# First attention of a four-layer network: dense masked products or nine shifted products on channel planes

## The reference

```python
def _unfold(x, k, dil):
    pad = dil * (k - 1) // 2
    xp = jnp.pad(x, ((0, 0), (0, 0), (pad, pad), (pad, pad)))
    return jnp.stack([xp[:, :, i * dil:i * dil + H, j * dil:j * dil + W] for i in range(k) for j in range(k)], axis=2)

def _dilate_attention(q, k, v, head_dim, scale, ksz, dil):
    qr = q.reshape(B, nh, head_dim, L)
    kp = _unfold(k, ksz, dil).reshape(B, nh, head_dim, kk, L)
    vp = _unfold(v, ksz, dil).reshape(B, nh, head_dim, kk, L)
    attn = jnp.einsum('bncl,bnckl->bnlk', qr, kp) * scale
    attn = jax.nn.softmax(attn, axis=-1)
    out = jnp.einsum('bnlk,bnckl->bnlc', attn, vp)
    ...
for g in range(G):                      # G = 4 groups of 48 channels
    qkv = jnp.einsum('oi,bihw->bohw', qkv_w, xg[g]).reshape(nd, 3, B, gd // 3, H, W)
    for i in range(nd):                 # dilations 1, 2, 3
        outs.append(_dilate_attention(qkv[i, 0], qkv[i, 1], qkv[i, 2], hd, scale, KSZ, DILATIONS[i]))
y = jnp.stack(outs).reshape(B, H, W, C)
return y @ proj_w.T + proj_b
```

## Time and profile before

| | us |
|---|---|
| runs of the kernel | 774.72, 776.76, 777.01 |
| median | 776.76 |
| span of the profiled execution | 779.2 |
| TensorE busy, share of the span | 707.0, 91% |
| VectorE, ScalarE, GpSimd busy | 392.7, 301.7, 227.0 |
| the block of the first attention, from its first product to that of the next block | 95.2 |

### The profile page before, as it was taken

One profiled execution on the slowest core, in us unless ns is written; L12 is line 12 of the kernel. 1 busy time (PEld: TensorE's weight loads), 2 busy tenths in 40 slices (PEclk: granted clock), 3 DMA queues, 4 the chain that ended last, 5 costly groups with the idle time before them and its releaser, 6 DMA issues. The chain is left out here.

```text
span 779.2 us, 14121 instructions
## 1 busy us (share of the span) xinstructions
PE 707.0 (91%) x4658; PEld 612.0 (79%) x4658; DVE 392.7 (50%) x983; ACT 301.7 (39%) x604; POOL 227.0 (29%) x271
## 2 busy tenths in 40 slices
PE   4987988999998999998888988899999896999997
PEld 2566767897796899995676778699999666777996
DVE  4466746015345443335678756334435476875301
ACT  3334533332413344424444552233452253555323
POOL 4166620002100044442055301723344204531000
PEclk9989999899999999999979999989999998999999
DMA  3735540534106166533788403567772279850352
GB/s 92 197 107 150 143 115 22 142 102 121 30 1 179 45 167 167 127 48 71 207 203 217 102 17 117 156 156 167 185 174 28 55 188 236 227 121 1 101 135 70
DMA packets 94011, 95.22 MB, mean 122 GB/s; under 512 B 18881, under 2 KB 80213, under 8 KB 93945
## 3 DMA queue, kind: packets, MB, share of 16 engines
q1 hardware_dynamic: 80568, 75.11, 36.6%
q0 software_dynamic: 11712, 18.18, 11.4%
q10 hardware_dynamic: 1680, 1.28, 0.6%
HBM read 66.92 MB, written 27.84 MB: 122 GB/s over the span
## 5 line engine op out<-in xcount | busy, mean ns | idle before, releaser
L2130 POOL DMA_INDIRECT sum_scratch<-area,f_row_index x48 | 72.4, 1509 | 172.3 <-DVE area L2053 157.0
L917 DVE TENSOR_REDUCE neg_max<-psum 128x4 f32<-128x1024 f32 x72 | 88.0, 1222 | 32.9 <-PE psum L803 32.0
L1804 PE MATMUL psum<-w,area 128*112 128x192 f32 (+1 forms) x576 | 96.2, 326 | 0.0
L1804 PEld LDWEIGHTS psum<-w,area 128*112 128x112 f32 (+1 forms) x576 | 93.5, 183 | 0.0
L990 POOL TENSOR_TENSOR shift<-ident,neg_max 128x256 fp32r<-128x256 f32 x96 | 66.5, 704 | 89.1 <-DVE neg_max L917 57.4
L295 PE MATMUL psum<-ident 128*128 128x128 f32 x624 | 82.0, 289 | 5.1 <-issue 1.9
L295 PEld LDWEIGHTS psum<-ident 128*128 128x128 f32 x624 | 77.9, 204 | 7.2 <-issue 5.9
L815 PE MATMUL psum<-q_parts,k_parts 128*128 128x256 f32 x288 | 79.6, 306 | 0.3
L803 PE MATMUL psum<-k_parts,q_parts 128*128 128x256 f32 x288 | 56.0, 321 | 25.9 <-DMA k_parts<-k_scratch 15.0
L816 PE MATMUL psum<-shift,ones_r 128*128 128x256 f32 x288 | 75.2, 292 | 0.0
L803 PEld LDWEIGHTS psum<-k_parts,q_parts 128*128 128x128 f32 x288 | 42.7, 208 | 38.6 <-issue 20.7
(11 more groups left out here) (258 smaller groups left out, 1329.9 us busy)
## 6 DMA issues: line engine op xcount, KB each, us to landing
w<-in_f_w_dram SPq DMA_DIRECT2D x32, 576.0 KB, 5.0
w<-in_f_w_dram SPq DMA_DIRECT2D x16, 384.0 KB, 4.7
w<-in_f_w_dram SPq DMA_DIRECT2D x32, 192.0 KB, 5.0
q_parts<-q_scratch SPq DMA_DIRECT2D x32, 192.0 KB, 3.5
q_scratch<-area SPq DMA_DIRECT2D x22, 192.0 KB, 2.2
k_parts<-k_scratch SPq DMA_DIRECT2D x63, 64.0 KB, 3.1
q_parts<-q_scratch SPq DMA_DIRECT2D x32, 96.0 KB, 2.9
q_parts<-q_scratch SPq DMA_DIRECT2D x40, 64.0 KB, 3.2
```

The lines of the kernel that those rows point to most:

```text
L917: ins = dve.tensor_reduce(most, ps[:, 0:2, :].rearrange("p b (c k) -> p (b c) k", c=2), AX_X, ALU.max, negate=True)
L1804: ins = pe.matmul(out, x.hidden[:, fc, R * c:R * (c + 1)], net.w2[:, b, fc, :], start=(fc == 0), stop=(fc == FCH - 1))
L2130: pool.indirect_dma_start(net.sum_dram[:, :], bass.IndirectOffsetOnAxis(ap=row_index[0:size, b, c:c + 1], axis=0), x.y[0:size, b, c, :], N ...
```

## The change

The first attention gets a block of its own, `near_attention`, with channels on partitions all the way (64 channels of a group for each of two images = 128 partitions). Per image pair n and group g:

- TensorE projects query and key, then the values; ScalarE copies them into planes, keys and values into planes with a zero border.
- For each row shift dy there are three column shifts, in one instruction: query times the shifted keys, 3 x 256 elements. VectorE takes dy = 0 and 1, GpSimd dy = 2.
- TensorE sums each product over the 16 channels of a head with a 0/1 matrix (`gather`), in four strips of 32 columns, one for each quarter of the tokens; three groups add up in the same banks.
- VectorE takes off the maximum, ScalarE exp, VectorE divides by the sum: one softmax for each image pair, 576 elements on 128 partitions.
- For each of 18 units (n, g, dy): TensorE spreads the weights of a head over its 16 channels (`spread`, strips of 32 rows), VectorE multiplies them from PSUM with the shifted values, in two halves of 3 x 128 elements; GpSimd adds two of the three column shifts; TensorE takes the sum and the third as stationary operands against the identity and adds up all of a group's nine, turned to tokens on partitions (`collect`).
- ScalarE copies out, SyncE stores to `o_scratch` and reads back as before; images 2 and 3 are now both read back in the next block.

The memsets of `q_parts`, which the later layers need, move from `load_input` behind GpSimd's last add; `load_input` clears the bordered planes instead. The loads of `prep.third` are all issued by SyncE at the start of the block. `attention` loses its branches for `m.local`.

```diff
-            nc.gpsimd.memset(net.q_parts[32:64, :, :].bitcast(F32), 0.0)
-            nc.gpsimd.memset(net.q_parts[64:128, :, :].bitcast(F32), 0.0)
+            nc.gpsimd.memset(near.padded, 0.0)
...
+def query_times_keys(eng, out, n, g, dy):
+    query = near.query[:, g, n, :].rearrange("p (s a b) -> p s a b", s=1, a=SIDE).to_broadcast([P, 3, SIDE, SIDE])
+    return eng.tensor_tensor(out.rearrange("p s (a b) -> p s a b", a=SIDE), query,
+                             window(near.keys, g, n, dy, 0, SIDE), ALU.mult)
...
+        @block.tensor
+            def channels(kind, g, n, out):
...
+                for k in range(2):
+                    i = 2 * n + k
+                    for c in chunks:
+                        ins = pe.matmul(out[64 * k:64 * (k + 1)], m.w[:, c, at:at + 64],
+                                        net.x_chan[:, c, IMG_TOK * i:IMG_TOK * (i + 1)],
+                                        start=(c == chunks[0]), stop=(c == chunks[-1]))
...
+            def gather(n, g, dy):
+                if dy == 1:
+                    u = vector_unit(n, g, dy)
+                    pe.wait_ge(product_by_vector, u + 1)
+                    products = near.by_vector[:, u % RING - 1:u % RING + 1]
+                else:
+                    pe.wait_ge(product_by_pool, n * GROUPS + g + 1)
+                    products = near.by_pool[:, g:g + 1]
+                rows = 3 - dy
+                for q in range(4):
+                    out = ps[32 * q:32 * (q + 1), LOGIT_BANKS[n][dy - 1], 0:256 * rows].rearrange("p (a x) -> p a x", a=rows)
+                    ins = pe.matmul(out[:, :, 0:3 * QUARTER].rearrange("p a (s t) -> p a s t", s=3), near.gather[:, g, :],
+                                    products[:, :, :, QUARTER * q:QUARTER * (q + 1)], start=(g == 0), stop=(g == GROUPS - 1))
+                ins.then_inc(gathered, 1)
+
+            def spread(n, g, dy, half):
+                w = unit(n, g, dy)
+                need(pe, weighted, 2 * (w - 1) + half + 1)
+                for q in (2 * half, 2 * half + 1):
+                    out = ps[:, SPREAD_BANKS[half][q % 2], :].rearrange("p (r x) -> p r x", r=4)[:, :, 0:3 * SIDE]
+                    ins = pe.matmul(out.rearrange("p r (s b) -> p s r b", s=3), near.spread[32 * q:32 * (q + 1), g, :],
+                                    near.probs[n][32 * q:32 * (q + 1), 3 * dy:3 * dy + 3, :].rearrange("p s (r b) -> p s r b", r=4),
+                                    start=True, stop=True)
+                ins.then_inc(spread_ps, 1)
+
+            def collect(n, g, dy):
+                w = unit(n, g, dy)
+                pe.wait_ge(weighted, 2 * w + 2)
+                if dy == 0:
+                    need(pe, mixed_sb, 2 * (n * GROUPS + g))
+                for s in (2, 0):
+                    products = near.by_vector[:, w % RING, s, :].rearrange("p (t x) -> p x t", x=2)
+                    if s == 0:
+                        pe.wait_ge(summed, w + 1)
+                    for t in range(2):
+                        ins = pe.matmul(ps[:, OUT_BANKS[t], 0:P], products[:, t, :], net.ident[:, :],
+                                        start=(dy == 0 and s == 2), stop=(dy == 2 and s == 0))
+                ins.then_inc(out_ps, 1)
...
+            for g in range(GROUPS):
+                for dy in (1, 2):
+                    gather(1, g, dy)
+                if g < 1:
+                    for job in range(2, 4):
+                        values(job)
+            units = [(n, g, dy) for n in range(2) for g in range(GROUPS) for dy in range(3)]
+            for w in range(len(units) + 2):
+                if w < len(units):
...
+                    for half in range(2):
+                        spread(n, g, dy, half)
+                if w >= 2:
+                    collect(*units[w - 2])
...
+        @block.vector
+            def weigh(n, g, dy):
...
+                for half in range(2):
...
+                    dve.wait_ge(spread_ps, 2 * w + half + 1)
+                    dve.tensor_tensor(out, probs.rearrange("p r (s b) -> p s r b", s=3),
+                                      window(near.values, g, n, dy, SIDE // 2 * half, SIDE // 2), ALU.mult).then_inc(weighted, 1)
...
+            for g in range(GROUPS):
+                for dy in range(2):
+                    product(0, g, dy)
+            for dy in range(2):
+                product(1, 0, dy)
+            less(0)
+            for dy in range(2):
+                product(1, 1, dy)
+            divide(0)
+            for dy in range(2):
+                product(1, 2, dy)
+            for g in range(GROUPS):
+                for dy in range(3):
+                    weigh(0, g, dy)
+                if g == 0:
+                    less(1)
+                if g == 1:
+                    divide(1)
...
+        @block.gpsimd
+            for n, g in NEAR_JOBS:
+                pool.wait_ge(taken, 2 * (n * GROUPS + g) + 2)
+                if n == 1:
+                    pool.wait_ge(gathered, 2 * g + 2)
+                query_times_keys(nc.gpsimd, near.by_pool[:, g], n, g, 2).then_inc(product_by_pool, 1)
+            nc.gpsimd.tensor_tensor(net.x_res[:, :, :], net.x_res[:, :, :],
+                                    m.pb[:, :, :].to_broadcast([P, TILES, D]), ALU.add)
+            for w in range(2 * GROUPS * 3):
+                products = near.by_vector[:, w % RING]
+                pool.wait_ge(weighted, 2 * w + 2)
+                nc.gpsimd.tensor_tensor(products[:, 0, :], products[:, 0, :], products[:, 1, :], ALU.add).then_inc(summed, 1)
+            pool.wait_ge(summed, 2 * GROUPS * 3)
+            nc.gpsimd.memset(net.q_parts[32:64, :, :].bitcast(F32), 0.0)
+            nc.gpsimd.memset(net.q_parts[64:128, :, :].bitcast(F32), 0.0)
```

More of the change, by code:

```diff
@@ L506, with attention @@
 KEY = 3
[L509 removed]
+def attention(net, m):
     nc, ps, tag = net.nc, net.psum, m.tag
@@ L971, in _ @@
                 pass
-            for g in range(2 - behind, GROUPS):
+            for g in range(1, GROUPS):
                 finish(IMGS - 1, g)
@@ L1026, in _, with __init__, take @@
                 pass
+class Near:
+    RING = 4
+    def __init__(self, net):
+        area = net.area
+        sides = [SIDE + 2 * (g + 1) for g in range(GROUPS)]
+        at = 0
+        self.keys, self.values = [], []
+        for kind in (self.keys, self.values):
+            for side in sides:
+                kind.append(area[:, at:at + 2 * side * side].rearrange("p (n a b) -> p n a b", n=2, a=side))
+                at += 2 * side * side
+        self.padded = area[:, 0:at]
+        def take(size):
+            nonlocal at
+            at += size
+            return area[:, at - size:at]
+        self.query = take(GROUPS * 2 * IMG_TOK).rearrange("p (g n t) -> p g n t", g=GROUPS, n=2)
+        self.logits, self.probs = ([take(9 * QUARTER).rearrange("p (s t) -> p s t", s=9) for _ in range(2)] for _ in range(2))
+        self.most, self.total = ([take(QUARTER) for _ in range(2)] for _ in range(2))
+        self.gather = take(GROUPS * 32).rearrange("p (g r) -> p g r", g=GROUPS)
+        self.spread = take(GROUPS * P).rearrange("p (g c) -> p g c", g=GROUPS)
+        each = "p (r s t) -> p r s t"
+        self.by_vector = net.w1[:, :, :, :].rearrange("p b k f -> p (b k f)").rearrange(each, r=self.RING, s=3)
+        self.by_pool = net.w2[:, :, :, :].rearrange("p b k f -> p (b k f)").rearrange(each, r=3, s=3)
```

422 lines of the change are left out of this document (241 added, 181 removed).

## The result

The changed kernel takes 754.54 us (median of four runs, 751.82 to 755.31) against 776.88 us, a ratio of 0.9719 with a 95% interval of 0.967 to 0.9768. The forecast was 755.0, its range 740 to 770.

What follows compares the result with a forecast made beforehand. The prediction took TensorE's products to bound the first attention's block. The next block would begin at 88.8 instead of 110.4 us, so 21.6 us off 776.8 gives 755 us, range 740 to 770.

Steps and rivals of the forecast that it cites:

- the softmax beside the queue: Scores: first image pair's division (0.7 us) and uncovered softmax steps, named beside the queued products; their end taken as 41.5 us.
- the unit of weighing: Each of 18 units takes 1.9 us on TensorE: paired spreads, collecting 1.0, and 0.2 for changes of form.
- the block behind: The blocks after the first attention should be as long as before; a change over 1 us means a missing step.
- queue of VectorE and GpSimd: Scores: instructions with two SBUF operands queue, 24.3 us in a row; twelfth product ends at 41.5, bounds 32.5 and 42.5.
- The projection: Start of the attention at 14.4 us; first job 1.7 us if its halves run side by side; first product near 17.2.
- rival A: Scores: VectorE and GpSimd do not hold each other up; twelfth product ends at 32.5, total 746 us; chance 0.15.
- From the twelfth product to the first weighing: Last gathers some 1.9 us, with the first spread and its latency 2.8; weighing begins near 44.3 us.
- Weighing: The 18 units: 33.5 us, plus 2.5 for the slow clock at the start and 2 for softmax, ending near 82.3.
- Rival B: Weighing: row strips don't pair, a unit takes 2.65 us, total 768 us; chance 0.20.
- Behind weighing: End of the block: GpSimd's memsets, 5.3 us, set the end, costing some 3; next block at 88.8, read-back hidden.
- C: Weighing: TensorE at its lower clock throughout and strips unpaired, 5.1 us a unit, total 809 us; chance 0.03.
- D: Weighing: slow clock but paired strips, 3.6 us a unit, total 784 us; chance 0.05.

Runs made afterwards that it cites:

- e2_allvec: The changed kernel with all 18 products of queries and keys on VectorE, GpSimd's add to x_res behind them: 749.13 us.
- e12_layout: The changed kernel with exponentials laid out by query, the nine terms of a sum side by side: 757.82 us in one run.
- e5_double: The changed kernel with every spreading instruction issued twice, 16 in a unit instead of 8: 758.37 us.
- e9_fill: The changed kernel with products that nobody reads ahead of the first spreads and in the first two units: 754.21 us.
- e10_softmax: The changed kernel with VectorE's second softmax spread, one instruction each behind units 3, 4, 6, 7 and 8: 755.51 us.
- e1_mem: The changed kernel with GpSimd's two memsets of q_parts right behind its add to x_res, not at the block's end: 750.31 us.
- e6_end: The changed kernel with 14 products that nobody reads behind TensorE's last collection: 750.11 us.
- e4_split: The changed kernel with each unit's spreads and collecting split into alternating halves, four changes of form instead of two: 787.57 us.

## Why the prediction was right

Its total, 755.0 against 754.54, is closer than its steps. Three of them were off by more than a microsecond: the softmax beside the queue, the unit of weighing, and the block behind. They were off to both sides; that the total came within half a microsecond is luck. What was right is the mechanism: fewer products on TensorE, a queue of VectorE and GpSimd, and weighing bound by TensorE.

**The projection held.** The attention began at 14.46 (14.4), the halves of a job ran side by side, VectorE's first product came at 17.16 (17.2).

**The queue of VectorE and GpSimd held,** and rival A fell (e2_allvec). But the twelfth product ended at 42.9, not 41.5, and so outside its bound of 42.5. The term that failed is the softmax beside the queue: 17.2 + 24.3 are 41.5, so the sum has nothing for it, although the text names it. The maximum and its subtraction did lie beside GpSimd's last product. But GpSimd was through at 37.9; behind that VectorE still had a division of 2.5 us and two products, and nothing of it lay beside other work. The division itself was priced at 1.7 (behind the sixth unit): the sum took 1.17 where neighbours take 0.74 (e12_layout), and the reciprocal 0.55. The latter is in the groups by line (mean ns of one ahead of the last bar):

```profile
L340 DVE RECIPROCAL rstd<-std 128x2 f32<-128x2 f32 x32 | 4.6, 143 | 4.1 <-ACT std L401 4.1
L1200 DVE RECIPROCAL area<-area 128x64 f32<-128x64 f32 x2 | 1.1, 554 | 0.1
```

Two elements take 0.14 us and 64 take 0.55, some 6.6 ns an element; beside two steps of 0.76 the 1.7 leave it 0.2, the price of a small one.

**From the twelfth product to the first weighing** it took 3.3 us, not 2.8: both the gathers (2.15) and the spreads (1.02) ran at the lower clock. The 1.9 for the gathers was a slip: at the spacing of the earlier trace rows, 0.23 us for 256 columns, two batches of 384 and two of 192 at half the clock are 2.1.

**Weighing** took 34.5 us on VectorE, from 46.2 to 80.7, not 38.0. The unit costs 1.75, not 1.9: the strips run four at a time where I had them paired, the collecting takes 1.1 instead of 1.0, and the way in and out some 0.3 instead of 0.2. Rival B fell (e5_double). Beside its pairs the prediction quotes 3.07 for four strips from the Trainium skill (TensorE: Matmul & The Clock Gate, Part 3) and says that the sum would be the paired one; by that figure the spreads are 1.43 / 3.07 = 0.47 us, an estimate between the 0.72 that it took and the 0.3 that e5_double shows. The start cost 3.7 us, not 4.5, and of this the clock is the larger part: with the clock held, the time from the first spreads to the last is 2.6 us shorter (e9_fill, 2.5 forecast), with the softmax spread 1.5 (e10_softmax, 2 forecast).

**Behind weighing** all was as forecast but earlier: two memsets of 2.65 us, the next block 0.5 behind them, at 87.42 instead of 88.8; they cost 2.7 us (e1_mem) where 3 were taken. In the next block TensorE has no wait for images 2 and 3: their read-back stayed hidden.

**A step was missing.** That the next block should be as long as before was the condition, and it was named as one; it was 1.8 us longer (12.9 against 11.1): 0.9 in its first 8 products and 0.9 in its first 16 of 192 columns. TensorE came to it after 4.67 us of idling, and the clock was at 0.50 up to 95 us; with the clock at 1.00 the block took 9.4 (e6_end). So the sentence that nothing outside the block depends on how the block does its work was wrong. I had taken the clock into account at the start of weighing and not behind it.

So + 1.4 for the queue, + 0.5 for the first spreads, - 3.5 for weighing, + 0.2 at its end give the 1.4 us by which the next block began early, and its own 1.8 us take them back.

**The cliff.** Rivals C and D, TensorE at its lower level through all of weighing, got 0.08 together. The mechanism is real: e4_split is the changed kernel with its instructions in another order, and it came out 1.6% slower than before, at 787.6 us where D had 784. The changed kernel's own clock rose between 54 and 55 us, over 9 us after its first spreads; in e1_mem it rose at 46 and was down again from 49 to 52. That it rises at all was argued from the old block's long products, which say little about units that change form all the time, and no run shows what lets it rise there. The nearest rows of before go into column strips and back between full-array products of 256 columns, in a block at a mean clock of 0.95; they say nothing of units as short as these. In the change's four runs the mean clock of the whole execution was 0.951 to 0.960, in e4_split's 0.915 to 0.921, so the clock rose in each of the four. That leaves open how near the changed kernel stands to the cliff, and 0.08 was a guess.

## What to carry to other kernels

Before giving part of VectorE's work to GpSimd, look whether both read two operands from SBUF. If so, the two don't add up; here the slower engine took nearly its whole time out of the faster one. When an engine is relieved, look at what it does at the borders of the stage: here 4.67 us of idle TensorE cost the next stage its clock, and 14 products that nobody reads won back 3.5 us of it in the trace. Where row strips and full-array products alternate, put as much as possible between two changes of form: the same instructions with twice as many changes were slower than the old kernel.

## What the runs showed of the hardware

- A product of 768 elements from two SBUF operands took VectorE 0.88 to 0.91 us with GpSimd idle or in a memset, and 1.83 on average beside GpSimd's products; two beside its add took 5.30.
- Four row strips ran at once: eight more instructions of 192 columns cost 0.3 us, against 1.43 one behind the other. A trip into strips and out cost an estimated 0.2 to 0.6 us, the most where it was made twice a unit.
- TensorE's clock stayed at 0.50 for 60 us in which no other engine was waited for, with four changes of form a unit; with four more products a unit it stayed there, with sixteen more it went to 1.00.
- VectorE read 576 single elements of SBUF, 9 or 64 apart, in 1.13 to 1.17 us, neighbours in 0.74 to 0.76, and elements 64 apart in PSUM in 0.76; ScalarE wrote elements 9 apart in 1.29 instead of 0.68.
